# Eight landing places for query tiles, zeroing in paced pairs, an earlier second block, and reordered first and last stages in an attention and mixture-of-experts kernel

## What is computed

```python
def _layernorm(x): return (x - mean(x)) / sqrt(var(x) + 1e-5)
x = x + attn(_layernorm(x))     # one causal head of width 1024: q, k, v = x W + b, scores / 32
x = x + ffn(_layernorm(x))
# ffn: router softmax over 8 experts, the best 2 of them by their probability;
#   routed = sum_e c[n, e] * (silu(x w1[e]) w2[e])
#   shared = sigmoid(x wg) * ((silu(x Wgate) * (x Wup)) Wdown)
```

## Time and profile before

| | |
|---|---|
| median of 3 runs | 1327.98 us (1326.18 to 1399.11) |
| the profiled execution | 1321.63 us |
| its span on core 5, the slowest | 1320.1 us (other cores 1296.0 to 1319.4) |
| TensorE busy in the span | 1148.1 us, 87% |
| VectorE, ScalarE, GpSimd busy | 580.8, 466.2, 269.6 us |
| DMA moved | 222.84 MB, mean 169 GB/s |

### The profile page before, as it was taken

How to read it: one execution, slowest core, us unless ns; L and a number is a source line. 1 busy time by engine, 2 the same in 40 slices (tenths; PEclk the granted TensorE clock), 3 DMA queues, 4 the chain that set the end, 5 groups by cost and what they waited for, 6 DMA issues and landing times.

```text
span 1320.1 us, 18840 instructions; the slowest of 8 cores (1296.0 to 1320.1 us)
## 1 busy us (share of the span) xinstructions
PE 1148.1 (87%) x6360; PEld 584.1 (44%) x6360; DVE 580.8 (44%) x1273; ACT 466.2 (35%) x900; POOL 269.6 (20%) x443
## 2 busy tenths in 40 slices
PE   4887899869989989898878669699996999999887
PEld 1454565324434434343333224244563666665433
DVE  3455336436657656566574744311011111111566
ACT  0344234315444544445454534412331222232200
POOL 4104001310122022121121022350011222211431
PEclk8888899989999999899998889799998999999988
DMA  9729725986786775778779395599199999999977
GB/s 178 181 52 222 174 41 128 212 182 126 144 179 148 150 183 136 167 161 156 160 148 184 73 138 103 89 178 151 46 237 215 204 213 212 223 207 207 323 264 260
DMA packets 248540, 222.84 MB, mean 169 GB/s; under 512 B 186868, under 2 KB 193140, under 8 KB 248440
## 3 DMA queue, kind: packets, MB, share of 16 engines
q0 software_dynamic: 52976, 129.02, 46.3%
q1 hardware_dynamic: 195464, 92.55, 33.0%
HBM read 172.25 MB, written 51.38 MB: 169 GB/s over the span
## 4 chain that ended last, share of the span: by engine, by line
PE 55%; DMA 18%; DVE 10%; ACT 7%; issue 5%; SPq 3%; POOL 1%; DVEq 0%; ACTq 0%; POOLq 0%
PE po L634 11%; PE sp L571 8%; PE sp L1137 7%; PE po L1162 7%; PE sp L819 7%; DMA PT<-P 5%; PE po L1222 4%; PE po L513 4%; DMA xn<-G 3%; DMA XT<-XN 3%; PE po L695 2%; DVE per_unit L589 2%; DMA O<-xkv 2%; ACT P L601 2%; DMA Y<-ys 2%
## 5 line engine op out<-in xcount | busy, mean ns | idle before, releaser
L634 PE MATMUL po<-XN,PT 128*128 128x512 bf16 x1088 | 261.0, 395 | 41.1 <-DMA PT<-P 29.4
L571 PE MATMUL sp<-XT,QT 128*128 128x512 bf16 x1088 | 256.6, 389 | 38.5 <-DMA XT<-XN 36.4
L634 PEld LDWEIGHTS po<-XN,PT 128*128 128x128 bf16 x1088 | 108.5, 101 | 186.1 <-issue 72.6
L571 PEld LDWEIGHTS sp<-XT,QT 128*128 128x128 bf16 x1088 | 105.9, 100 | 168.9 <-issue 54.0
L1175 DVE COPY ys<-po 128x1024 f32<-128x1024 f32 x35 | 42.9, 1225 | 230.7 <-PE po L1162 211.2
L819 PE MATMUL sp<-QT,WGU 128*128 128x512 bf16 x512 | 116.9, 389 | 6.5 <-DVE HB L834 6.5
L647 DVE SCALAR_TENSOR_TENSOR O<-O,per_unit,po 128x512 f32<-128x512 f32 x112 | 80.4, 742 | 51.2 <-PE po L634 48.9
L599 ACT ACTIVATE per_unit<-nm,s_q 128x1 f32<-128x1 f32 x72 | 21.4, 297 | 225.8 <-DVE nm L596 111.8
L1144 ACT ACTIVATE hT<-sp 128x640 bf16<-128x640 f32 x64 | 45.1, 705 | 113.4 <-PE sp L1137 113.4
L69 POOL DMA_DIRECT2D xs<-xkv x60 | 32.5, 545 | 255.3 <-ACT XN L278 226.3
L589 DVE TENSOR_REDUCE per_unit<-sp 128x1 f32<-128x1024 f32 (+1 forms) x72 | 83.5, 1159 | 2.0 <-DVE sp L587 0.5
(11 more groups left out here) (152 smaller groups left out, 1361.1 us busy)
## 6 DMA issues: line engine op xcount, KB each, us to landing
Y<-ys SPq DMA_DIRECT2D x40, 512.0 KB, 9.0
O<-xkv POOLq DMA_DIRECT2D x64, 256.0 KB, 6.4
xs<-xkv POOLq DMA_DIRECT2D x60, 256.0 KB
G<-zero POOLq DMA_DIRECT2D x16, 640.0 KB, 9.4
xn<-G SPq DMA_DIRECT2D x8, 1280.0 KB, 20.9
xr<-xkv POOLq DMA_DIRECT2D x16, 512.0 KB, 4.8
W<-w1p POOLq DMA_DIRECT2D x32, 256.0 KB, 17.6
W<-w2p POOLq DMA_DIRECT2D x32, 256.0 KB, 21.1
```

What stands on the lines that cost most here:

```text
L571: fn = lambda e, d=d, h=h: e.matmul(sp[j][:, h * 512:h * 512 + 512], QT[:, d * 2048 + t * 128:d * 2048 + t * 128 + 128], XT[kb % 2][:, h * ...
L634: fn = lambda e, c=c, h=h, i=i: e.matmul(ring[i], PT[p][:, c * 128:c * 128 + 128], XN[kb % 2][:, c * 1024 + h * 512:c * 1024 + h * 512 + 5 ...
```

## The change

It has four parts. (1) Own tiles 4 to 11 get a landing place each, O8 to O15, and are loaded as soon as the key tile that lay there is normed and the last weight chunk has landed; tiles 12 to 15 reuse O8 to O11. (2) Six of the sixteen zeroing DMAs are issued before unit 0; the other ten go in pairs at units 3 to 7, each pair behind a wait for that unit's scores. The eighths of WV stay at units 10 to 17, without a zeroing DMA between them. (3) Block 1's jobs use six places at once (x0, x1, O12 to O15), are normed from unit 7 on (five steps per unit), and their DMA transpositions are emitted two per unit at units 10 to 13. (4) In the first stage the five transpositions on TensorE move from the first half of M to the second, row 7 of both halves comes last, and own tiles 2 and 3 are normed before projection 0. In the last stage eight low rows are added first, then one low row ahead of each of the tiles 0 to 7, and gathers are issued in the order of use.

```diff
-    own_keys = [("x", 0), ("x", 1)] + [("O", t) for t in range(8, 12)] * 3
+    own_keys = [("x", 0), ("x", 1)] + [("O", t) for t in range(8, 16)] + [("O", t) for t in range(8, 12)]
...
-                        [(d_wk[7].sem, 16)] if t < 8 else [])
-    keys1 = [("x", 0), ("x", 1), ("O", 15), ("O", 14), ("x", 0), ("x", 1), ("x", 0), ("x", 1)]
+                        [(d_wk[7].sem, 16)] if t < 12 else [])
+    keys1 = [("x", 0), ("x", 1), ("O", 12), ("O", 13), ("O", 14), ("O", 15), ("x", 0), ("x", 1)]
...
-    for chain in ([kv[1, 0], kv[1, 4], kv[1, 6]], [kv[1, 1], kv[1, 5], kv[1, 7]],
-                  *[[kv[0, j], own[j + 4], own[j + 8], own[j + 12]] for j in range(4)]):
+    for chain in ([kv[1, 0], kv[1, 6]], [kv[1, 1], kv[1, 7]],
+                  *[[kv[0, j], own[j + 4]] + ([own[j + 12]] if j < 4 else []) for j in range(8)]):
...
-    turn_at = {3: [0], 5: [1], 6: [2], 7: [3]}
     for c in range(8):
         PE.wait((d_wq[c].sem, 32))
         for r in range(7):
             mm_m(0, r, r, c)
-        for i in turn_at.get(c, []):
-            free7 = pe_turn(lead[i], 7, free7)
     m_free = [evict_m(0, r, r, r % 2) for r in range(7)]
-    free7 = pe_turn(lead[4], 7, free7)
+    for c in range(8):
+        PE.wait((d_wk[c].sem, 16))
+        for r in range(7):
+            if c == 0:
+                PE.wait(m_free[r])
+            mm_m(1, r, r, c)
+        if c < 5:
+            free7 = pe_turn(lead[c], 7, free7)
...
-    PE.wait(free7)
-    for c in range(8):
-        mm_m(0, 7, 7, c)
-    free7 = evict_m(0, 7, 7, True)
-    for c in range(8):
-        PE.wait((d_wk[c].sem, 16))
-        for r in range(7):
-            if c == 0:
-                PE.wait(m_free[r])
-            mm_m(1, r, r, c)
...
-    PE.wait(m_free[0])
-    for c in range(8):
-        mm_m(1, 7, 0, c)
+    for h in range(2):
+        PE.wait(m_free[h])
+        for c in range(8):
+            mm_m(h, 7, h, c)
...
-    k_M7 = evict_m(1, 7, 0, True)
-    k_Mv, k_Ma = m_free[6], k_M7
-    m_free[0], free7 = k_M7, k_b0
+    m_free[0] = evict_m(0, 7, 0, True)
+    m_free[1] = evict_m(1, 7, 1, False)
+    k_Mv, k_Ma, free7 = m_free[1], m_free[0], k_b0
+    for jb in second[3:]:
+        ln_stats(jb)
+        ln_norm(jb, True)
...
-    last_steps = ln_steps([kv[1, j] for j in range(8)])
+    last_steps = []
+    for j in range(9):
+        last_steps += [lambda j=j: ln_stats(kv[1, j])] if j < 8 else []
+        last_steps += [lambda j=j: ln_norm(kv[1, j - 1], False)] if j > 0 else []
...
+    zero_tok = [None]
+
+    def zero_part(i):
+        zero_tok[0] = POOL.dma(lambda e: e.dma_start(
+            out=G[i * CAP // 2:(i + 1) * CAP // 2, :].rearrange("(s p) d -> p s d", p=64),
+            in_=zero[0:64, :].unsqueeze(1).broadcast_to([64, CAP // 128, 1024])), d_zero, k_zeroed)
...
-    for jb in second[3:]:
-        ln_stats(jb)
-        ln_norm(jb, True)
+    for i in range(6):
+        zero_part(i)
...
-        if 2 <= x < 18:
-            k_zero = POOL.dma(lambda e, i=x - 2: e.dma_start(
-                out=G[i * CAP // 2:(i + 1) * CAP // 2, :].rearrange("(s p) d -> p s d", p=64),
-                in_=zero[0:64, :].unsqueeze(1).broadcast_to([64, CAP // 128, 1024])), d_zero, k_zeroed)
+        if 3 <= x < 8:
+            POOL.wait(qk_tok[x])
+            zero_part(2 * x)
+            zero_part(2 * x + 1)
+        if 10 <= x < 18:
             w = slice((x - 10) * 1024, (x - 9) * 1024)
-            if x >= 10:
-                k_wv[0] = POOL.dma(lambda e, w=w: e.dma_start(out=WV[:, w], in_=wvh[:, w]), d_wv, proj_done[7])
+            k_wv[0] = POOL.dma(lambda e, w=w: e.dma_start(out=WV[:, w], in_=wvh[:, w]), d_wv, proj_done[7])
...
         if x == 5:
-            for j in range(4):
+            for j in range(6):
                 ln_load(kv[1, j], POOL)
...
-                if x >= 8:
-                    n = -(-len(last_steps) // max(1, 15 - x))
-                    for s in last_steps[:n]:
+                if x >= 7:
+                    for s in last_steps[:5]:
                         s()
-                    last_steps = last_steps[n:]
+                    last_steps = last_steps[5:]
+                if 10 <= x < 14:
+                    ln_turn(kv[1, 2 * x - 20])
+                    ln_turn(kv[1, 2 * x - 19])
...
     def gather(t, side, rows, *after):
-        b = (side * NT + t) % 6
+        b = g_n[0] % 6
+        g_n[0] += 1
...
+    rows = [(t, 0) for t in range(8)]
     for t in range(NT):
-        b, k = gather(t, 0, 7 * CAP, *y_low, k_low, k_lohi)
-        add_row(t, 0, b, k)
+        rows += [(8 + t, 0)] if t < 8 else []
+        rows += [(t - 2, 1)] if t >= 2 else []
+    rows += [(NT - 2, 1), (NT - 1, 1)]
+    asked, taken_ = [], [0]
+
+    def add_rows(n):
+        for _ in range(n):
+            while len(asked) < min(len(rows), taken_[0] + 5):
+                t, side = rows[len(asked)]
+                asked.append(gather(t, side, *((8 * CAP, *y_free) if side else (7 * CAP, *y_low, k_low, k_lohi))))
+            t, side = rows[taken_[0]]
+            add_row(t, side, *asked[taken_[0]])
+            taken_[0] += 1
+
+    add_rows(8)
     SPE.wait(k_dw)
     for t in range(NT + 2):
+        if t < 8:
+            add_rows(1)
...
         if t >= 2:
-            b, k = gather(t - 2, 1, 8 * CAP, *y_free)
-            add_row(t - 2, 1, b, k)
+            add_rows(1)
```

More of the change, by code:

```diff
@@ L481, in build_program @@
                                             op0=ALU.mult))
-    k_M7 = evict_m(1, 7, 0, True)
-    k_Mv, k_Ma = m_free[6], k_M7
-    m_free[0], free7 = k_M7, k_b0
+    m_free[0] = evict_m(0, 7, 0, True)
[4 more added lines that the diff above has]
+        ln_norm(jb, True)
     sp_free = [m_free[0], m_free[3]]
-    sp_wait0 = [m_free[1], m_free[2]]
+    sp_wait0 = [m_free[0], m_free[1], m_free[2], m_free[3]]
     ring_free = [m_free[4], m_free[5], m_free[6]]
@@ L791, in retire_d @@
                 out=G[:, :], out_offset=bass.IndirectOffsetOnAxis(ap=posu[:, 2 * t + c:2 * t + c + 1], axis=0),
-                in_=xf[i][:], in_offset=None), d_sc[i], a, ret[t]["xf"], k_zero)
+                in_=xf[i][:], in_offset=None), d_sc[i], a, ret[t]["xf"], zero_tok[0])
         xf_free[i] = [scattered[i], xf_turned[t]]
@@ L886, in build_program @@
             step(t)
-        if 2 <= x < 18:
-            k_zero = POOL.dma(lambda e, i=x - 2: e.dma_start(
-                out=G[i * CAP // 2:(i + 1) * CAP // 2, :].rearrange("(s p) d -> p s d", p=64),
-                in_=zero[0:64, :].unsqueeze(1).broadcast_to([64, CAP // 128, 1024])), d_zero, k_zeroed)
+        if 3 <= x < 8:
[3 more added lines that the diff above has]
+        if 10 <= x < 18:
             w = slice((x - 10) * 1024, (x - 9) * 1024)
-            if x >= 10:
-                k_wv[0] = POOL.dma(lambda e, w=w: e.dma_start(out=WV[:, w], in_=wvh[:, w]), d_wv, proj_done[7])
+            k_wv[0] = POOL.dma(lambda e, w=w: e.dma_start(out=WV[:, w], in_=wvh[:, w]), d_wv, proj_done[7])
         if x == 18:
-            xr_free[0] = k_zero
+            xr_free[0] = zero_tok[0]
             POOL.wait(own[3]["turned"])
@@ L1194, in build_program @@
     g_free = [None] * 6
+    g_n = [0]
     def gather(t, side, rows, *after):
-        b = (side * NT + t) % 6
+        b = g_n[0] % 6
+        g_n[0] += 1
         return b, SPOOL.dma(lambda e: e.indirect_dma_start(
```

## The result

The changed kernel takes 1322.51 us (median of 20 runs, 1313.79 to 1361.53), the kernel before in the same job 1337.65 (20 runs). In some executions of any of these kernels the cores of a die show a lower granted clock and take longer; they count in the medians and are left out of every ratio. The ratio is 0.9927 [0.9899, 0.9955] (in brackets the 95% interval). That is faster by 0.7%, and "same" by the prediction's own line of two per cent. 1322.5 lies outside the forecast range: 41 us were forecast, about 10 came. The profiled execution took 1316.97 us; its slowest core is core 1 with a span of 1315.4.

The account below looks back on a forecast made before the run. It took TensorE's waits on DMA, and on VectorE itself held by DMA, as the bound. Gains of 9.4, 28.9 and 3 us, together 41.3, gave 1287 us from the median 1327.98; range 1271 to 1308.

Parts of the forecast that it names:

- part 2: Block 0: waits on loads, P and transposed blocks mostly go, gaining 28.9 us, bounds 12 and 36.
- It fits: Unit 5: P leaves 14.6 us after the scores, is needed at 21.2, so the 5.55 us wait and 2.65 go.
- rival B: Block 0: block 1 loads with zeroing, and unpaced value weights, each hold a P 10 us more; 1307 us, chance 0.20.
- The unpaced value weights: Block 0: eight issues drain in one go, making unit 11's P and the next late; 5 us lost with slow groups.
- Tiles 4 to 11 at once: Block 0: loads issued together near 50 us drain in a DMA-empty stretch; VectorE's 6.3 us wait for tile 8 goes.
- Block 1 earlier: Block 0: norms from unit 7, transposes from unit 10, so the 11.1 us wait before unit 17 goes.
- the 40.7 us: TensorE's loss from unit 1's scores to unit 15's values, 195.8 us against 155.1 of work; 11.8 was to remain.
- Part 1: Weight product before 90 us: 9.4 us gain, from 5.2 earlier first projection, 3.3 for norms ahead, 0.9 at unit 1's scores.
- Part 3: Last stage: the 12.6 us to win less 9.7 of new waits, a gain of 3 us, bounds -6 and +12.
- rival D: Last stage: gathers and outputs share a slow DMA rate, 159 GB/s giving 1346 us; chance 0.02.
- The middle: From 285 to 1240 us: counted unchanged, since TensorE and softmax order there are untouched.
- rival C: Middle: waits on DMA there give back a third of the gain; 1301 us, chance 0.09.

Follow-up runs that it names:

- e1: Changed kernel with the ten paced zeroing parts in pairs at units 8 to 12 instead of 3 to 7; 1313.99 us, ratio 0.9872 to the kernel before.
- e2: Changed kernel with block 1's six tiles loaded two each at units 4, 5 and 6 instead of six at unit 5; 1321.81 us, ratio 0.9955.
- e4: Changed kernel with zeroing at units 8 to 12, block 1 loads two each at units 4 to 6, value weights paced; 1309.14 us, ratio 0.986.
- e5: Changed kernel with block 1 loads spread, value weights paced, and ten zeroing parts three, four, three at units 7, 8, 9; 1283.95 us, ratio 0.9739.
- e3: Changed kernel with each eighth of the value weights waiting for its unit's scores at units 10 to 17; 1306.46 us, ratio 0.9825.
- e11: e5 with seven norm steps of own tiles instead of nine at units 0 and 1; 1312.08 us, ratio 0.9719 to the kernel before.
- e15: Kernel before with its zeroing alone moved: six parts before unit 0, ten at units 7 to 9; 1303.06 us, ratio 0.9809.
- e10: e5 with own tiles 2 and 3 normed behind projection 0, as before the change; 1291.34 us, ratio 0.9742 to the kernel before.
- e7: Kernel before with only the last stage of the change; 1325.07 us, ratio 1.0037.
- e8: Kernel before with only the first stage of the change; 1322.28 us, ratio 1.0013.
- e14: e9 with seven norm steps at units 0 and 1 in place of nine; 1283.79 us, ratio 0.971 to the kernel before.
- e9: e5 with each two zeroing parts as one 128-partition DMA; 1293.29 us, ratio 0.977 to the kernel before.

## Why the prediction was wrong

**Its failed step is one sentence of part 2, "It fits".** Unit 5's P did leave in time: forecast 14.6 us after the scores, it was issued 16.6 after them (142.1 to 158.71). It was given 6.6 us for its landing and took 26.98, and the wait of 22.64 is the prediction's own sign of being wrong, a P wait above 10. I had priced the stretch by volume at 288 GB/s, a rate at which zeroing and loads had drained together. I had also left out the pairs of units 6 and 7, issued at 157.10 and 163.97: with them 7.1 MB were to drain, by the same rate 24.6 us from 142.8, an estimate that has P some 4 us late and not 22.6. So leaving them out is the smaller part of the error, and the rate the larger. The trace of before had the warning in rows that I did not read, SyncE's list, core 5, beside the burst of the earlier trace rows:

```profile
130.31 2.03 SPq L618 DMA_TRANSPOSE PT<-P  x1
132.38 17.53 SPq L288 DMA_TRANSPOSE XT<-XN  x2
150.06 1.22 SPq L618 DMA_TRANSPOSE PT<-P  x1
151.32 2.67 SPq L288 DMA_TRANSPOSE XT<-XN  x2
```

The same pair of issues takes 17.53 us in the burst and 2.67 after it. The runs put in its place: beside XT transpositions, loads alone cost 0.9 us at most (e1) and a zeroing pair alone no wait (unit 4 of the changed kernel); zeroing and loads together 15 to 25 (changed kernel), 8 to 20 (e2), 10 to 16 (e1, at units 10 and 11) and 8 to 15 (e4); beside P's transpositions alone 8 or less (e5).

In the prediction's own stretch, from the end of unit 1's scores to unit 15's values, core 1 took 205.6 us (85.50 to 291.06), where 166.9 were forecast and 195.8 were taken before. Of the 38.7 that are missing, unit 5 has 24.1 (22.64 and the slow group's 1.4), the value weights 7.3, projection 2 some 7.0 and projection 1 some 2.2; small waits were 1.9 fewer than counted.

I had named the two bursts as rival B, at 10 us each and chance 0.20; the first was more than twice that, so B's 1307 was short as well (ratio 0.984; measured 0.9927).

**The unpaced value weights** were the second mis-sized term: 5 us counted, 8.35 and 2.01 of waiting and 1.9 of slow group on core 1, 12.3 in all. e3 takes them back. B's reason held for this one.

**Tiles 4 to 11 at once** went as forecast: the burst drained in the empty stretch. But the 6.3 us credited to it in the earlier trace rows were not all DMA: 4.4 stay with all tiles landed, and 3.75 with fewer norm steps (e11). Against its work of 7.37 us, projection 2 lost 8.0 us on core 1 and 6.7 on core 5, before 8.3 on core 5. VectorE's own steps were the limit close behind the load.

**Block 1 earlier** went as forecast in the changed kernel (the XT wait vanished, block 1 is 15 us shorter); e15 shows that on most cores the wait goes also if the zeroing alone is moved. There block 2 begins 25.8 us earlier than before, so that wait and the larger part of the 40.7 us went with the zeroing's place. I saw its parts in the earlier trace rows and read them as volume.

**Part 1**: first projection 3.8 us (changed) to 5.7 us (e4) earlier, forecast 5.2. The norms ahead held TensorE 3.7 us, not 1.7, and a wait of 2.9 in projection 1 and one of 4.4 in projection 2 remained. On core 5 unit 2's scores came 3.8 us earlier in place of 9.4. The 3.3 us for norms ahead were nothing (e10). The VectorE chain was costed for its place, not for its length.

**Part 3** was right as far as the profiles tell: forecast 3, measured 2 to 5; e7's ratio doesn't resolve it. Waits 6.1 us on core 1 for 9.7 forecast, the first high gather 8.2 us after the first shared tile for 12. DMA share 1.00 at 315 GB/s, forecast 330: the stretch became DMA's, and rival D's low rate did not come.

**The middle** (block 2 to first expert) was 526.0 us in the changed kernel, 532.8 before, 522.2 in e5: rival C fell. "Unchanged" was not right either. In e7 and e8, whose code there is that of before, it was 527.1 and 529.6, so some 6 us differ between profiles of the same code; the 10 us of e5 are more than that, and their cause stays open.

**What the forecast was worth**: 41 us forecast, ratio 0.969. With zeroing and value weights mended, e5 gives 0.9739 and e14 0.971. The sum was about right for a kernel in which the zeroing is not in the way, but partly by luck: in the profiles (medians over the cores) e5 reaches block 2 26.8 us earlier where 38.3 were forecast, and the middle gave 10.6 that were not counted.

**Open.** Why zeroing, loads and XT transpositions hurt together and no two of them so much. The three were not varied one by one at one unit: zeroing beside XT alone was seen at unit 4 only, whose P has a projection more of room than unit 5's. XT's are issued in pairs behind a P, so that three follow at once, and this was not varied either. How much of e5's gain is the slack of the projections at units 7 to 9. How much of e14's lead over e15 (0.971, 0.9809) is real.

## What to carry to other kernels

Price a burst not by its bytes alone but by what is in flight beside it: beside transpositions of tiles, 3.1 MB of loads cost 0.9 us at most, a 1.3 MB pair of zeroing parts (at another unit) no wait, and loads and zeroing together 22 us. Before adding landing places and an earlier stage, move the suspected transfer by itself; here that gave 1.9% where the whole change gave 0.7%. And where a wait is put down to a load, ask what the engine's own list would still hold if the load were free.

## What the runs showed of the hardware

At share 1.32 the DMA engines moved 95 GB/s (changed kernel, core 1, 170 to 180 us), with transpositions, zeroing and tile loads issued shortly before; ten microseconds earlier they moved 315. The issue of a transposition on SyncE, 1.2 us when quiet, took 12 us, and that of a pair up to 22: the engine that issues is held, and the next P behind it in its list with it, 20 us in e4. Added to the same loads and transpositions at unit 5, zeroing of 1.3 MB a unit gave a wait of 24.84, 11.14 or 6.34 us by its form (two DMAs of 64 partitions, one of 64, one of 128; core 5, one profile each). Where no tile was being transposed, ten parts in 31 us gave waits up to 8.0 us in the first form (e5) and up to 0.8 in the last (e9).
